# A gated cross-attention block on one core: the third chunk's keys moved ahead of the first slot, and the fourth chunk's transform one slot on

## The chip, the cores and the metric

The kernel runs on one core of one Trainium2 chip. The metric is the device time of one execution in microseconds; before the change it is 108.18 us, the median of three runs (108.13 to 108.33). All stretches of time below are in microseconds from the start of the profiled span.

## What is computed

The input `x` is 8 sequences of 128 tokens with 256 channels. Each token passes two gated branches:

```
x = x + tanh(g_xattn[0]) * wkv(w, u, k=layernorm(x), v=ctx)
x = x + tanh(g_ffn[0])   * ffn(layernorm(x))
```

`wkv` is a recurrence over the 128 tokens of a sequence: a numerator p (decayed sum of exp(k)*v) and a denominator q (decayed sum of exp(k)), and an output y = (A p + E v) / (A q + E). `ffn` applies signs and a normalised Walsh-Hadamard transform to its 256 inputs, multiplies by `W_up` and `W_gate` (1024 x 256 each), forms silu(gate) * up, applies signs and a second Hadamard transform to these 1024 values, and multiplies by `W_down` (256 x 1024).

## The kernel before

**Tiling.** Channels and hidden units lie on the partitions, tokens on the free axis. The 1024 tokens are four chunks of 256 (`NG` = 4, two sequences each), and the 1024 hidden units are eight tiles of 128. A *slot* q is one hidden tile of one chunk, so there are 32 slots; chunk g has the slots 8g to 8g+7. In a slot the PE (TensorE) runs `up(q)` (lines 962 to 1009: 12 matmuls into one PSUM bank, gate and up halves side by side; three products of a high part and a low part in place of one fp32 product), ACT (ScalarE) takes silu of the gate half into S (`gate`, line 636) and, one slot later, the high part of H (`hi`, line 630), DVE (VectorE) multiplies into H (`hidden`, line 815), and POOL (GpSimd) takes the low part HL (line 490). Six slots later (`LAG`) the PE runs `down(q - 6)`, 6 matmuls that add the tile's contribution to the output sums. The banks UG0 to UG3 are used in turn, so `up(q)` waits until H of slot q - 4 is done (`wait_bank_free`, line 275).

**What comes before a chunk's slots.** For each chunk: the layer norm of X (`stats1`, `rstd1` on POOL at line 456, `norm1`), `keys` (PE turns the normalised X and adds a term linear in time, lines 851 to 875; ACT takes exp of the result, line 561), two scans on DVE (line 683), the quotient, x1 = x + branch (line 777), the transform F of x1 (`fwht` on the PE, lines 925 to 943, from the high and low parts XH and XL of x1), squares on ACT, their sum over the channels (`sum` on POOL at line 483, `ones` on the PE at lines 944 to 960, into VB), an inverse square root RR by Ln and Exp on ACT (`rstd2`), a Newton step on DVE in VB whose last operation writes RB (`root`, lines 780 to 788), and F scaled by RB (`f_scaled`, line 792), of which ACT takes the high part FH (line 628) and DVE the low part FL (line 797). `up` of the chunk's first slot waits for FH and FL. The first chunk's `y_part` at line 895 stands for its transform. The scaled F lies in PSUM, its left half in the right half of VB and its right half in FX (`scaled`, line 338).

**Other steps near the change.** `w n` turns a piece of the weights into UGn (line 917), `w_hi` and `w_rest`, `w_lo` split it into two parts (lines 587, 924, 591); `m a` transforms a piece of the down weights into KZ, VB or OD (line 908), from pieces that POOL prepared (`fly`, line 387). `warm` and `warm_ug` are matmuls whose result nobody reads.

**What sets the order.** Four tables (`PE_STAGES` and so on, lines 44 to 102) list by hand which steps each engine issues after which slot; -1 is the part before slot 0. Each engine issues in that order and waits on semaphores. In the table a step is a name and a number: a chunk for `keys`, `fwht`, `ones`, `square`, `sum`, `norm1`; a piece for `w`, `m`. On ACT the Ln and Exp of a chunk stand in an `exp_block` with a table load ahead (line 575) and one behind (line 578), since silu needs another table.

Of the kernel before, what the change touches and what calls it, by code (L numbers as in the profile page):

```python
# [14 lines left out]
CT = C // P  # L15
# [3 lines left out]
GT = GB * P  # L19
# [23 lines left out]

PE_STAGES = {
    -1: [("warm", 9), ("keys", 0), ("warm", 5), ("center", 0), ("w", 0), ("warm", 1), ("x_part", 0), ("w", 1), ("w_rest", 0), ("w", 2),
        ("y_part", 0), ("keys", 1), ("ones", 0), ("w_rest", 1), ("w", 3), ("w_rest", 2), ("m", 0), ("warm_ug", 1)],
    0: [("w_rest", 3)],
    1: [("keys", 2), ("m", 1)],
    2: [("m", 2)],
    3: [("m", 3), ("fwht", 1)],  # L50
    4: [("keys", 3), ("ones", 1)],
    9: [("fwht", 2)],
    12: [("ones", 2)],
    17: [("fwht", 3)],
    19: [("ones", 3)],
}
ACT_STAGES = {
    -1: [("setup", 0), ("own", 0), ("decay", 0), ("signs", 0), ("keys", 0), ("weighted", 0), ("signs", 1), ("ratio", 0), ("negative", 0), ("minus", 1),
        ("center", 0), ("recip", 0), ("w_hi", 0), ("norm1", 1), ("w_hi", 1), ("w_lo", 0), ("w_hi", 4), ("square", 0), ("keys", 1), ("minus", 2), ("w_hi", 2),
        ("rstd2", 0), ("w_lo", 1), ("w_hi", 3), ("w_lo", 2), ("f_hi", 0), ("m_hi", 0), ("norm1", 2), ("recip", 1), ("w_hi", 5), ("w_lo", 3), ("keys", 2)],  # L60
    1: [("m_hi", 1), ("w_hi", 6), ("x_hi", 1)],
    2: [("m_hi", 2), ("w_hi", 7)],
    3: [("m_hi", 3), ("square", 1)],
# [2 lines left out]
    9: [("square", 2)],  # L66
    12: [("exp_block", (("rstd2", 2), ("recip", 3))), ("f_hi", 2)],
    15: [("x_hi", 3)],
    17: [("square", 3)],
    19: [("exp_block", (("rstd2", 3),)), ("f_hi", 3)],  # L70
}
DVE_STAGES = {
    -1: [("stats1", 0), ("setup_rows", 0), ("norm1", 0), ("setup_shift", 0), ("stats1", 1), ("outs", 0), ("scan_a", 0),
# [12 lines left out]
    12: [("root", 2), ("f_scaled", 2), ("f_lo", 2), ("estimate", 3)],  # L86
    13: [("newton", 3), ("x1", 3)],
    15: [("x_lo", 3)],
    19: [("root", 3), ("f_scaled", 3), ("f_lo", 3)],
}  # L90
POOL_STAGES = {
    -1: [("rstd1", 0), ("rstd1", 1), ("fly", 0), ("mix_den", 0), ("fly", 1), ("error", 0), ("fly", 4), ("fly", 2), ("fly", 3), ("fly", 6), ("rstd1", 2),
# [5 lines left out]
    6: [("x1_first", 0)],  # L98
    8: [("sum", 2)],
    11: [("error", 3)],  # L100
    17: [("sum", 3)],
}


# [42 lines left out]
def build(nc, x, xt, ct, rows, consts, weights, w_down, out):  # L147
    with ExitStack() as stack:
# [57 lines left out]
        UG = [bank(f"UG{i}") for i in range(NBANKS)]  # L206
        OD = bank("OD")
        KZ = bank("KZ")
        FX = bank("FX")
        VB = bank("VB")  # L210
# [126 lines left out]

        def scaled(g, t):

            return (FX if t else VB)[:, GT:2 * GT]  # L340

        def normalise(eng, g, done):

# [311 lines left out]
        def _(dve):  # L655
# [32 lines left out]
            def stage(name, g):  # L688
# [24 lines left out]
                elif name == "norm1":  # L713
                    normalise(dve, g, by_dve["norm1"])
                elif name == "av":
                    multiply_values(dve, g, by_dve["av"])
                elif name == "scan_a":
                    dve.wait_ge(decay_set, CT)
                    dve.wait_ge(pads, 2)
                    if g:  # L720
                        dve.wait_ge(den_ready, g)
                    dve.wait_ge(a_ready, g + 1)
                    scan(SQ, g, OD[:, :] if g in HELD else EA[:, g - len(HELD), :, :, :].rearrange("p t b q -> p (t b q)"), scanned_a)
                elif name == "scan_av":
                    if g:
                        dve.wait_ge(num_ready, g)
                    wait_shared(dve, "av", g)
                    scan(SP_, g, OD[:, :] if g in HELD else V[:, g, :, :, :].rearrange("p t b q -> p (t b q)"), scanned_v)
                elif name == "mix_den":
                    if g == 2:  # L730
                        dve.wait_ge(y_first, CT)
                    elif g > 2:
                        dve.wait_ge(y_ready, g - 2)
                    dve.wait_ge(scanned_a, 2 * g + 2)
                    for t in range(CT):
                        i = dve.scalar_tensor_tensor(out=DEN[:, g % 2, t, :, :], in0=exps(g)[:, t, :, :], scalar=RATIO[:, t:t + 1],
                                                     in1=states(SQ)[:, t, :, :], op0=ALU.mult, op1=ALU.add)
                    i.then_inc(den_ready, 1)
                elif name == "mix_num":
                    if g == 0:  # L740
                        dve.wait_ge(ratio_ready, 1)
                    dve.wait_ge(scanned_v, 2 * g + 2)
                    num = values(g)
                    for t in range(CT):
                        i = dve.scalar_tensor_tensor(out=num[:, t, :, :], in0=num[:, t, :, :], scalar=RATIO[:, t:t + 1],
                                                     in1=states(SP_)[:, t, :, :], op0=ALU.mult, op1=ALU.add)
                    i.then_inc(num_ready, 1)
                elif name == "error":
                    reciprocal_error(dve, g, by_dve["error"])
                elif name == "estimate":  # L750

                    dve.wait_ge(r0_ready, g + 1)
                    dve.wait_ge(num_ready, g + 1)
                    if g:
                        dve.tensor_tensor(lanes(values(g)), lanes(values(g)), lanes(R0[:, g % 2, :, :, :]), ALU.mult).then_inc(y0_ready, 1)  # L755
                    else:
                        dve.wait_ge(tanh_gate, 1)
                        dve.scalar_tensor_tensor(out=lanes(values(g)), in0=lanes(values(g)), scalar=TG[:, 0:1], in1=lanes(R0[:, g % 2, :, :, :]),
                                                 op0=ALU.mult, op1=ALU.mult).then_inc(y0_ready, 1)
                elif name == "newton":  # L760

                    wait_shared(dve, "error", g)
                    dve.wait_ge(y0_ready, g + 1)
                    if g:
                        dve.scalar_tensor_tensor(out=lanes(values(g)), in0=lanes(DEN[:, g % 2, :, :, :]), scalar=2.0, in1=lanes(values(g)),
                                                 op0=ALU.subtract, op1=ALU.mult).then_inc(y_ready, 1)
                    else:
                        for t in range(CT):
                            dve.scalar_tensor_tensor(out=YT[:, t, :].rearrange("p (b q) -> p b q", b=GB), in0=DEN[:, 0, t, :, :], scalar=2.0,
                                                     in1=values(g)[:, t, :, :], op0=ALU.subtract, op1=ALU.mult).then_inc(y_first, 1)  # L770
                elif name == "x1":

                    dve.wait_ge(y_ready, g)
                    dve.wait_ge(tanh_gate, 1)
                    dve.wait_ge(xt_in[arrival(g)], 16)
                    xg = XT[:, g, :, :].rearrange("p t (b q) -> p (t b) q", q=P)
                    dve.scalar_tensor_tensor(out=xg, in0=lanes(values(g)), scalar=TG[:, 0:1], in1=xg, op0=ALU.mult, op1=ALU.add).then_inc(x1_ready, 1)
                elif name == "x_lo":
                    split_x1(dve, g, by_dve["x_lo"])
                elif name == "root":  # L780

                    var = VB[:, 0:GT]
                    dve.wait_ge(rr_ready, g + 1)
                    dve.scalar_tensor_tensor(out=var, in0=var, scalar=EPS * C, in1=RR[:, :], op0=ALU.add, op1=ALU.mult).then_inc(e_ready, 1)
                    dve.wait_ge(e_ready, 3 * g + 1)
                    dve.tensor_tensor(var, var, RR[:, :], ALU.mult).then_inc(e_ready, 1)
                    dve.wait_ge(e_ready, 3 * g + 2)
                    dve.scalar_tensor_tensor(out=RB[:, :], in0=var, scalar=3.0, in1=RR[:, :], op0=ALU.subtract, op1=ALU.mult).then_inc(e_ready, 1)
                elif name == "f_scaled":
                    dve.wait_ge(e_ready, 3 * g + 3)  # L790
                    for t in range(CT):
                        dve.scalar_tensor_tensor(out=scaled(g, t), in0=FX[:, t * GT:(t + 1) * GT], scalar=-0.5, in1=RB[:, :],
                                                 op0=ALU.mult, op1=ALU.mult).then_inc(f_scaled, 1)
                elif name == "f_lo":
                    for t in range(CT):
                        dve.wait_ge(f_hi, CT * g + t + 1)
                        dve.tensor_tensor(FL[:, g, t, :], scaled(g, t), FH[:, g, t, :].bitcast(F32), ALU.subtract).then_inc(f_lo, 1)
                elif name == "fly":
                    fly(dve, g, by_dve["fly"])
                elif name == "w_lo":  # L800
                    split_weight(dve, g, by_dve["w_lo"])
                elif name == "m_lo":
                    dve.wait_ge(m_hi, M_HI.index(g) + 1)
                    dve.tensor_tensor(m_part(ML, g), fill(("m", g))[:, :], m_part(MH, g).bitcast(F32), ALU.subtract).then_inc(by_dve["m_lo"], 1)
# [36 lines left out]
        def _(pe):  # L841
            def stage(name, g):
# [8 lines left out]
                elif name == "keys":  # L851
# [5 lines left out]
                    else:  # L857
                        pe.wait_ge(a_ready, g)
                    if g == 2:
                        pe.wait_ge(f_lo, CT)  # L860
                    elif g == 3:
                        wait_shared(pe, "m_lo", M_FULL[1])
                    keys = VB if g == 2 else KZ
# [234 lines left out]
```

## Time and profile before

| | |
|---|---|
| runs | 108.13, 108.18, 108.33 us |
| the profiled execution | 108.13 us; its span 106.2 us |
| PE busy | 100.4 us (94%), 724 matmul records |
| weight load (PEld) | 91.3 us (86%) |
| DVE | 70.0 us (66%) |
| ACT | 68.4 us (64%) |
| POOL | 62.4 us (59%) |
| PE's share of the chain that ended last | 60% |
| mean granted TensorE clock | 0.999 of 2.4 GHz |

An engine's rows give the start and the duration; of several merged instructions the duration reaches from the first start to the last end. Matmuls overlap their neighbours, so the time that one takes from the PE is the distance between starts, not its duration.

### The profile page before, as it was taken

To read this page: it belongs to the slowest core of one execution; us is meant where nothing else is said; L and a number is where in the kernel's file an instruction comes from. 1 tells how busy PE (TensorE), PEld (TensorE's weight loads), DVE (VectorE), ACT (ScalarE), POOL (GpSimd) and SP (SyncE) were. 2 spreads that over 40 slices of the span, in tenths; PEclk is the share of its full clock that TensorE was granted. 3 is DMA by queue.
4 is the path that set the end of the run, shared out by engine and by line. 5 is a ranking of instruction groups with operands and counts; after the bars stand their busy time and mean duration, and the time that the engine had idled before them with its cause. 6 is when DMAs were issued, how large, how long until landed. Compare 5 with 4: busy or idle time off the path is not lost.

```text
span 106.2 us, 2028 instructions
## 1 busy us (share of the span) xinstructions
PE 100.4 (94%) x724; PEld 91.3 (86%) x724; DVE 70.0 (66%) x151; ACT 68.4 (64%) x153; POOL 62.4 (59%) x74
## 2 busy tenths in 40 slices
PE   6999999989999999988999999799999999999990
PEld 5778778659667999978999999699999999999980
DVE  0388889799899996898998269942298231125221
ACT  4098797989979699925346997565976432443400
POOL 7025999996999995049996345455208234225500
PEclk9999999999999999999999999999999999999999
DMA  1999999300000000000000000020000200000202
GB/s 59 271 348 398 413 413 405 147 0 9 0 0 0 0 6 0 0 0 3 0 0 6 0 0 0 0 105 0 0 0 3 99 6 0 0 0 3 99 6 99
DMA packets 2893, 7.70 MB, mean 72 GB/s; under 512 B 321, under 2 KB 706, under 8 KB 2754
## 3 DMA queue, kind: packets, MB, share of 16 engines
q1 hardware_dynamic: 2882, 7.56, 19.0%
q8 instruction: 6, 0.10, 0.4%
q14 instruction: 5, 0.04, 0.1%
HBM read 6.51 MB, written 1.05 MB: 71 GB/s over the span
## 4 chain that ended last, share of the span: by engine, by line
PE 60%; DVE 13%; ACT 9%; issue 6%; POOL 5%; DMA 3%; DVEq 0%; ACTq 0%; POOLq 0%
PE UG L978 33%; PE OD L1016 8%; DMA X<-in_x 3%; PE KZ L1016 3%; PE FX L941 3%; PE VB L1016 3%; PE FX L1016 3%; PE FX L895 2%; DVE XL L377 2%; PE KZ L908 2%; PE OD L908 2%; PE VB L908 2%; DVE BS L706 1%; POOL RS L456 1%; DVE V L755 1%
## 5 line engine op out<-in xcount | busy, mean ns | idle before, releaser
L490 POOL TENSOR_TENSOR HL<-H,HH 128x256 fp32r<-128x256 f32 x32 | 25.5, 805 | 27.5 <-ACT HH L634 27.5
L826 DVE SCALAR_TENSOR_TENSOR H<-S,ALPHA,UG 128x256 f32<-128x256 f32 x32 | 15.0, 476 | 16.7 <-ACT S L643 16.6
L643 ACT ACTIVATE S<-UG,HI 128x256 f32<-128x256 f32 x32 | 15.0, 471 | 13.7 <-PE UG L978 13.7
L978 PE MATMUL UG<-FH,WTH 128*128 128x256 f32 x128 | 21.7, 292 | 0.8 <-DVE H L826 0.5
L634 ACT ACTIVATE HH<-H 128x256 fp32r<-128x256 f32 x32 | 13.2, 414 | 10.9 <-DVE H L826 10.9
L978 PE MATMUL UG<-FH,WTL 128*128 128x256 f32 x128 | 19.9, 278 | 0.0
L978 PE MATMUL UG<-FL,WTH 128*128 128x256 f32 x128 | 19.9, 278 | 0.0
L978 PEld LDWEIGHTS UG<-FH,WTH 128*128 128x128 f32 x128 | 17.6, 188 | 2.6 <-issue 1.7
L978 PEld LDWEIGHTS UG<-FH,WTL 128*128 128x128 f32 x128 | 17.1, 188 | 0.0
L978 PEld LDWEIGHTS UG<-FL,WTH 128*128 128x128 f32 x128 | 17.0, 188 | 0.0
L849 PE MATMUL VB<-ONES 128*128 128x256 f32 x30 | 10.0, 499 | 1.0 <-POOL ONES L439 1.0
L849 PEld LDWEIGHTS VB<-ONES 128*128 128x128 f32 x30 | 7.5, 260 | 2.5 <-POOL ONES L439 1.0
L1016 PE MATMUL OD<-HL,MH 128*128 128x256 f32 x32 | 8.9, 278 | 0.0
L1016 PE MATMUL OD<-HH,ML 128*128 128x256 f32 x32 | 8.9, 278 | 0.0
L1016 PE MATMUL OD<-HH,MH 128*128 128x256 f32 x32 | 8.9, 278 | 0.0
L364 POOL TENSOR_TENSOR DEN<-DEN,R 128x512 f32<-128x512 f32 x4 | 5.1, 1283 | 4.7 <-ACT R L572 4.7
L456 POOL TENSOR_TENSOR RS<-VE,NHALF 128x2 f32<-128x2 f32 x4 | 2.8, 704 | 5.8 <-DVE VE L712 5.8
L370 POOL TENSOR_TENSOR WTL<-WN,WTH 128x512 fp32r<-128x512 f32 x4 | 6.1, 1517 | 0.0
L1016 PEld LDWEIGHTS OD<-HL,MH 128*128 128x128 f32 x32 | 6.0, 189 | 0.0
L1016 PEld LDWEIGHTS OD<-HH,ML 128*128 128x128 f32 x32 | 6.0, 188 | 0.0
L1016 PEld LDWEIGHTS OD<-HH,MH 128*128 128x128 f32 x32 | 6.0, 188 | 0.0
L706 DVE BATCH_NORM_STATS2 BS<-X 128x6 f32<-128x256 f32 x8 | 3.0, 414 | 4.2 <-DMA X<-in_x 4.2
(159 smaller groups left out, 221.6 us busy)
## 6 DMA issues: line engine op xcount, KB each, us to landing
WN<-in_weights SPq DMA_DIRECT2D x4, 512.0 KB, 9.2
DN<-in_w_down SPq DMA_DIRECT2D x1, 1024.0 KB, 6.8
out<-XT SPq DMA_DIRECT2D x3, 256.0 KB, 2.5
X<-in_x SPq DMA_DIRECT2D x2, 256.0 KB, 3.8
V<-in_ct SPq DMA_DIRECT2D x2, 256.0 KB, 7.7
XT<-in_xt SPq DMA_DIRECT2D x2, 256.0 KB, 9.3
X<-in_x SPq DMA_DIRECT2D x1, 512.0 KB, 9.3
V<-in_ct SPq DMA_DIRECT2D x1, 512.0 KB, 11.7
```

What stands on the lines that cost most here:

```text
L364: eng.tensor_tensor(lanes(DEN[:, g % 2, :, :, :]), lanes(DEN[:, g % 2, :, :, :]), lanes(R0[:, g % 2, :, :, :]), ALU.mult).then_inc(done, 1)
L370: eng.tensor_tensor(w_part(WTL, n), src, w_part(WTH, n).bitcast(F32), ALU.subtract).then_inc(done, 1)
L456: pool.tensor_tensor(RS1[:, GB * g:GB * (g + 1)], VE1[:, GB * g:GB * (g + 1)], NHALF[:, :], ALU.pow).then_inc(rstd1, 1)
L490: pool.tensor_tensor(HL[:, q % JT, 0:n], ring(H, q), HH[:, q % JT, 0:n].bitcast(F32), ALU.subtract).then_inc(h_lo, 1)
L634: act.activation(HH[:, q % JT, 0:n], ring(H, q), ACT.Copy).then_inc(h_hi, 1)
L643: act.activation(ring(S, q), gate_part(q), ACT.Silu, scale=VT[:, V_SGATE + j:V_SGATE + j + 1]).then_inc(silu_ready, 1)
L706: dve.bn_stats(BS1[:, n, :], X[:, n, :]).then_inc(stats1, 1)
L826: dve.scalar_tensor_tensor(out=ring(H, q), in0=ring(S, q), scalar=ALPHA[:, j:j + 1], in1=up_part(q), op0=ALU.mult, op1=ALU.mult).then_inc( ...
L849: pe.matmul((VB if name == "warm" else UG[1])[:, 0:WARM].rearrange("p (k q) -> p k q", q=P), ONES[:, :], ONES[:, :].unsqueeze(1).broadcast ...
L908: a = pe.matmul(fill(item)[:, :], had, DN[:, n:n + 2, :].rearrange("p j c -> p (j c)"), start=(i == 0), stop=(i == 1), skip_group_check=True)
L978: return pe.matmul(dst.rearrange("p (g n) -> p g n", n=GT), w[:, m, j, t, :], f[:, chunks, t, :], start=start, stop=stop, skip_group_check ...
L1016: a = pe.matmul(total(g, t), m[:, j, t * P:(t + 1) * P], h[:, j, 0:n], start=(j == 0 and k == 0 and (t == 0 or g == LAST)), stop=(j == JT ...
```

## The change

It does four things. (1) On the PE, `keys` of the third chunk (number 2) moves from behind slot 1 to ahead of slot 0, the matmul `warm_ug` is gone, and `m 0` goes ahead of `w_rest 2`. On ACT, the normalisation of that chunk (`norm1` 2) moves from behind `m_hi 0` to directly behind `w_lo 1`, and `w_hi 3` and `w_lo 2` move behind `m_hi 0`. (2) The scaled F of the first chunk has its left half in UG1 in place of VB, and DVE waits for `w_lo` 1 before it writes there. (3) The keys of the third chunk wait for the end of the first chunk's Newton step (`e_ready` 3) in place of its low part FL. (4) The fourth chunk's `fwht`, `square` and `sum` go from behind slot 17 to behind slot 18, its `ones`, exponentials, Newton step, scaling and splits from behind slot 19 to behind slot 20.

```diff
 PE_STAGES = {
     -1: [...
-        ("y_part", 0), ("keys", 1), ("ones", 0), ("w_rest", 1), ("w", 3), ("w_rest", 2), ("m", 0), ("warm_ug", 1)],
+        ("y_part", 0), ("keys", 1), ("ones", 0), ("w_rest", 1), ("w", 3), ("m", 0), ("w_rest", 2), ("keys", 2)],
     0: [("w_rest", 3)],
-    1: [("keys", 2), ("m", 1)],
+    1: [("m", 1)],
...
-    17: [("fwht", 3)],
-    19: [("ones", 3)],
+    18: [("fwht", 3)],
+    20: [("ones", 3)],
 ACT_STAGES = {
...
-        ("rstd2", 0), ("w_lo", 1), ("w_hi", 3), ("w_lo", 2), ("f_hi", 0), ("m_hi", 0), ("norm1", 2), ("recip", 1), ("w_hi", 5), ("w_lo", 3), ("keys", 2)],
+        ("rstd2", 0), ("w_lo", 1), ("norm1", 2), ("f_hi", 0), ("m_hi", 0), ("w_hi", 3), ("w_lo", 2), ("recip", 1), ("w_hi", 5), ("w_lo", 3), ("keys", 2)],
...
-    17: [("square", 3)],
-    19: [("exp_block", (("rstd2", 3),)), ("f_hi", 3)],
+    18: [("square", 3)],
+    20: [("exp_block", (("rstd2", 3),)), ("f_hi", 3)],
 DVE_STAGES = {
...
-    19: [("root", 3), ("f_scaled", 3), ("f_lo", 3)],
+    20: [("root", 3), ("f_scaled", 3), ("f_lo", 3)],
 POOL_STAGES = {
...
-    17: [("sum", 3)],
+    18: [("sum", 3)],
...
         def scaled(g, t):
-            return (FX if t else VB)[:, GT:2 * GT]
+            if t:
+                return FX[:, GT:2 * GT]
+            return VB[:, GT:2 * GT] if g else UG[1][:, 0:GT]
...
                 elif name == "f_scaled":
                     dve.wait_ge(e_ready, 3 * g + 3)
+                    if g == 0:
+                        wait_shared(dve, "w_lo", 1)
...
                     if g == 2:
-                        pe.wait_ge(f_lo, CT)
+                        pe.wait_ge(e_ready, 3)
```

The PE's instructions from behind `w 3` to the start of slot 0, before:

```order
L924 MATMUL UG<-WTH,NI 128x512 [waits ni_ready,w_hi]
L908 MATMUL KZ<-DN,HI 128x512 [waits const_in,fly_pool,a_ready]
L908 MATMUL KZ<-DN,HI 128x512
L849 MATMUL UG<-ONES 128x256 [waits w_lo_act,ones_set]
L978 MATMUL UG<-FH,WTH 128x256 [waits f_hi,w_hi,w_lo_act]
```

and with the change (all lines of the kernel's code there are four further on):

```order
L912 MATMUL KZ<-DN,HI 128x512 [waits const_in,fly_pool,a_ready]
L912 MATMUL KZ<-DN,HI 128x512
L928 MATMUL UG<-WTH,NI 128x512 [waits ni_ready,w_hi]
L872 MATMUL VB<-HI,X 128x128 [waits norm1_act,e_ready,a_ready]
L872 MATMUL VB<-HI,X 128x128 x3
L878 MATMUL VB<-STEPR,WPLUS 128x256 x2
L982 MATMUL UG<-FH,WTH 128x256 [waits f_hi,w_hi,w_lo_act]
```

The four transposes and two matmuls of the keys now stand between `w_rest 2` and slot 0, where one matmul of ones stood, and the first of them waits for ACT's normalisation.

ACT from `w_lo 1` on, before:

```order
L591 ACTIVATE WTL<-UG 128x512
L587 ACTIVATE WTH<-UG 128x512
L591 ACTIVATE WTL<-UG 128x512
L628 ACTIVATE FH<-VB 128x256
L628 ACTIVATE FH<-FX 128x256
L595 ACTIVATE MH<-KZ 128x512
L547 ACTIVATE NMR<-NM,RS 128x1 x2
L551 ACTIVATE X<-X,NMR,RS 128x256 x2
L570 ACTIVATE R<-DEN 128x512
```

and with the change:

```order
L593 ACTIVATE WTL<-UG 128x512
L549 ACTIVATE NMR<-NM,RS 128x1 x2
L553 ACTIVATE X<-X,NMR,RS 128x256 x2
L630 ACTIVATE FH<-UG 128x256
L630 ACTIVATE FH<-FX 128x256
L597 ACTIVATE MH<-KZ 128x512
L589 ACTIVATE WTH<-UG 128x512
L593 ACTIVATE WTL<-UG 128x512
L572 ACTIVATE R<-DEN 128x512
```

The normalisation (NMR, X) and the two weight steps (WTH, WTL) have changed places around FH and MH.

The PE between slots 17 and 18, from the last matmul of `down(11)`, before:

```order
L1016 MATMUL KZ<-HL,MH 128x256
L941 MATMUL FX<-XH,AT 128x256 x4
L941 MATMUL FX<-XL,AT 128x256 x4
L978 MATMUL UG<-FH,WTH 128x256 x4
L978 MATMUL UG<-FH,WTL 128x256 x4
L978 MATMUL UG<-FL,WTH 128x256 x4
```

and with the change:

```order
L1020 MATMUL KZ<-HL,MH 128x256
L982 MATMUL UG<-FH,WTH 128x256 x4
L982 MATMUL UG<-FH,WTL 128x256 x4
L982 MATMUL UG<-FL,WTH 128x256 x4
L1020 MATMUL KZ<-HH,MH 128x256
```

The eight matmuls of the fourth chunk's transform now follow `up(18)` and `down(12)`.

## Rows read from the trace of the kernel before

**Rows 1.** The chain that ended last, in order of time: start, us, what.

```profile
22.05 0.44 DVE VB L792
...
24.70 0.23 PE UG L924
...
37.35 0.12 ACT S L643
```

**Rows 2.** Timeline of PE, 20 to 28: start, us, instruction [idle before <-releaser].

```profile
20.32 1.96 PE L908 MATMUL KZ<-DN,HI 128*128 128x512 f32 x4
22.11 0.59 PE L849 MATMUL UG<-ONES 128*128 128x256 f32 x2
23.04 0.74 PE L978 MATMUL UG<-FH,WTH 128*128 128x256 f32 x4 [0.34 <-ACT FH L628]
23.62 0.62 PE L978 MATMUL UG<-FH,WTL 128*128 128x256 f32 x4
...
26.18 0.60 PE L868 MATMUL VB<-HI,X 128*128 128x128 f32 x4
...
26.86 1.88 PE L908 MATMUL KZ<-DN,HI 128*128 128x512 f32 x4
```

**Rows 3.** Timeline of ACT, 21 to 25.

```profile
21.01 0.59 ACT L587 ACTIVATE WTH<-UG 128x512 fp32r<-128x512 f32 x1
...
22.52 0.38 ACT L628 ACTIVATE FH<-VB 128x256 fp32r<-128x256 f32 x1 [0.43 <-DVE VB L792]
...
23.61 0.47 ACT L547 ACTIVATE NMR<-NM,RS 128x1 f32<-128x1 f32 x2
23.97 1.08 ACT L551 ACTIVATE X<-X,NMR,RS 128x256 f32<-128x256 f32 x2
```

**Rows 4.** Timeline of POOL, at 20.

```profile
20.18 0.70 POOL L456 TENSOR_TENSOR RS<-VE,NHALF 128x2 f32<-128x2 f32 x1
```

**Rows 5.** Timeline of PE, 46 to 48.

```profile
46.95 0.74 PE L978 MATMUL UG<-FH,WTH 128*128 128x256 f32 x4 [0.47 <-DVE H L826]
47.52 0.62 PE L978 MATMUL UG<-FH,WTL 128*128 128x256 f32 x4
```

**Rows 6.** Timeline of DVE, 38 to 57.

```profile
38.69 1.58 DVE L745 SCALAR_TENSOR_TENSOR V<-V,RATIO,SP_ 128x256 f32<-128x256 f32 x2
...
41.59 0.43 DVE L784 SCALAR_TENSOR_TENSOR VB<-VB,RR 128x256 f32<-128x256 f32 x1 [0.92 <-ACT RR L624]
...
56.11 0.88 DVE L745 SCALAR_TENSOR_TENSOR V<-V,RATIO,SP_ 128x256 f32<-128x256 f32 x2
```

**Rows 7.** Timeline of PE, 67 to 73.

```profile
67.82 0.28 PE L1016 MATMUL KZ<-HL,MH 128*128 128x256 f32 x1
68.79 0.71 PE L941 MATMUL FX<-XH,AT 128*128 128x256 f32 x4 [0.70 <-ACT XH L601]
...
70.12 0.63 PE L978 MATMUL UG<-FH,WTH 128*128 128x256 f32 x4
...
72.17 0.62 PE L978 MATMUL UG<-FH,WTH 128*128 128x256 f32 x4
```

**Rows 8.** Timeline of DVE, at 67: H of slot 14.

```profile
67.21 0.47 DVE L826 SCALAR_TENSOR_TENSOR H<-S,ALPHA,UG 128x256 f32<-128x256 f32 x1
```

**Rows 9.** Timelines of POOL, PE and DVE, 73 to 83: the fourth chunk's sums, F, first slot.

```profile
73.30 0.74 POOL L483 TENSOR_TENSOR FSUM<-FSQ 128x256 f32<-128x256 f32 x1
...
74.21 0.64 PE L954 MATMUL VB<-FSUM,ONES 128*128 128x256 f32 x2
...
79.46 0.42 DVE L797 TENSOR_TENSOR FL<-FX,FH 128x256 fp32r<-128x256 f32 x1
...
82.88 0.62 PE L978 MATMUL UG<-FH,WTH 128*128 128x256 f32 x4
```

**Rows 10.** Timeline of PE, 0 to 8; then one line's records (ns min/median/max).

```profile
0.98 7.09 PE L849 MATMUL VB<-ONES 128*128 128x256 f32 x18 [0.98 <-POOL ONES L439]
...
L849 PE MATMUL UG<-ONES x2: 379/380/380, 22.1 to 22.3; 128*128 128x256 f32 x2
```

## The prediction

> **What bounds the kernel now.** The page first: the PE is busy for 94% of the span, and the slices where it is not are few. So the question at each place is whether the PE waits, and for whom. The chain that ended last answers it. Up to 22.5 it runs through DVE and ACT (the Newton step, then F scaled at 22.05, [rows 1]), and the PE is the one that waits: it stands idle for 0.34 us before slot 0, released by FH [rows 2]. From 23.04 the chain is the PE's alone until it reaches ACT's silu of slot 4 at 37.35 [rows 1]. There ACT has to get slot 4's gate before it may load the exp table, and the second chunk's F, and behind it everything up to about 50, hangs on that. From about 51 on it is the PE again, save for one wait: behind slot 17 the PE issues its last matmul at 67.82 and the next only at 68.79, because the fourth chunk's transform needs XH [rows 7]. After 70.12 the PE never waits.
>
> Hence two places at which the time can be moved: the work in the PE's queue between 23.04 and 37, where every microsecond taken out brings slot 4 forward, and the wait at 67.9.
>
> **Keys of the third chunk ahead of slot 0.** Their six instructions (the four transposes and two matmuls, of more records in the trace) take the PE from 26.18 to 26.86, 0.68 us, all of it on the chain [rows 2]. They leave that place. In the new place they follow `m 0` and `w_rest 2`. `m 0` cannot start earlier than its 20.32, as it did not wait for `w_rest 2` but for POOL's last piece, which ended when POOL began the next operation at 20.18, about 0.1 earlier [rows 2, 4]; it holds the PE until 22.11, and `w_rest 2` takes 0.23 as its neighbour does [rows 1, 2], so the PE is free at 22.34. The keys must also wait for ACT. ACT is free for the normalisation at 21.01, where `w_hi 3` started [rows 3]; its inputs from POOL are there at 20.18 + 0.70 = 20.88 [rows 4]. It takes 25.05 - 23.61 = 1.44 us [rows 3], to 22.45. FH started at 22.52 after an idle time of 0.43 [rows 3], so the normalisation just fits ahead of it, and FH is not late: what hides it is that idle time plus the 1.07 of the two weight steps that moved behind. The Newton step is done at 22.05, so the new wait of the keys on it costs nothing.
>
> From ACT's end to the PE's start the trace has 0.14 us (FH ends at 22.90, the PE starts at 23.04 [rows 2, 3]). The keys start at 22.45 + 0.14 = 22.59. A stream of matmuls that starts after idling loses something more: the first four of slot 9 took 0.57 [rows 5], where 18 matmuls of a slot take 72.17 - 70.12 = 2.05, so 0.114 each and 0.46 for four [rows 7]. That is 0.11 for a start, and it lies between 0 and 0.11 here, as the PE has idled for only 0.25 us. I take the 0.11, since slot 9's start, the nearest row, carries it. Then slot 0 starts at 22.59 + 0.68 + 0.11 = 23.38, against 23.04. It no longer pays for its own start: its first four took 23.62 - 23.04 = 0.58 [rows 2] and now take 0.46. So the PE is 0.34 - 0.12 = 0.22 late into slot 0 and 0.68 early behind slot 1: **0.46 us** gained, between 0.45 and 0.59. `warm_ug` stood in the PE's wait for FH (its start at 22.11 [rows 2]), and its removal brings nothing by itself.
>
> Does the gain reach the end? Between 26.2 and 37.3 the trace shows no wait of the PE, and with the queue 0.46 earlier the releases that I followed are still in time: DVE's XL of the second chunk by about 0.5 us, ACT's `w_hi 3`, now behind `m_hi 0`, by about 0.3 us before `w_rest 3`. Slot 4's silu comes 0.46 earlier, ACT's exp block with it, and DVE, which idled 0.92 us for RR at 41.59 [rows 6], has 0.46 of that left. From there on all is released by that chain, so it shifts as a whole.
>
> POOL gets its share earlier too, since ACT reaches the second chunk's reciprocal about 0.4 us sooner, and POOL's operations then lie otherwise beside DVE's. The same pair of DVE operations took 1.58 us at 38.69 and 0.88 at 56.11 [rows 6]; the difference of 0.70 bounds what a collision with POOL costs, and gain and loss are both open, from -0.70 to +0.70. Up to 0.46 of a loss goes into the idle time before 41.59, so at most 0.24 would be seen; I take nothing, as the pair at 38.69 bears its collision already. The Trainium skill (SBUF — State Buffer, Who interferes with whom) says that a DVE instruction with two SBUF inputs and a reading GpSimd instruction lock each other out for a whole instruction, by issue order. By that rule one more instruction of POOL in the way could cost its full length and would be seen as the same 0.2 to 0.3 us; the doubled pair agrees with it.
>
> **F's left half in UG1.** The same DVE and ACT operations on another PSUM bank, and a wait on `w_lo 1`, which ACT had all but ended when its next operation started at 21.01 [rows 3], while F is scaled at 22.05 [rows 1]: nothing. It is what makes VB free for the keys in time.
>
> **The fourth chunk's transform a slot on.** Behind `down(11)` the PE is free at 67.82 + 0.11 = 67.93, and slot 18 starts at 70.12: 2.19 us, of which eight matmuls at 0.114 need 0.91 [rows 7]. The rest, **1.28 us**, is the wait for XH and then XL. In the new order `up(18)` comes first. It waits for H of slot 14, done at 67.21 + 0.47 = 67.68 [rows 8], 0.25 before the PE is free, and a release by DVE is seen some 0.05 later. The transform starts at 67.93 + 2.05 = 69.98, when XH and XL have long been there: before, all of it had been issued by 70.12. So the whole 1.28 goes, if nothing else comes late.
>
> What is late next? Sums: the PE's `ones` follows the transform by two slots before and now, and POOL's sum by the same steps, done at 74.04 for a start at 74.21 [rows 9]; the margin of 0.17 stays. The F of the fourth chunk: the `ones`, and ACT's and DVE's block, come one slot (2.05) later and 1.28 earlier, so 0.77 later: FL at 79.46 + 0.42 + 0.77 = 80.65. Slot 24 now asks for it at 82.88 - 1.28 = 81.60 [rows 9]. 0.95 us are left. ACT's silus of slots 21 to 23 wait behind the block instead of 20 to 22, and the PE asks for slot 21's H only at slot 25. No DMA is moved, and no instruction but the matmul of ones is added or removed.
>
> **The sum.** 0.46 + 1.28 = 1.74. The profiled execution took 108.13 us, 1.9 more than its span, and 0.05 below the median; 108.13 - 1.74 = 106.39, against the median 106.44. I say **106.4 us**.
>
> **The rivals.**
>
> *The first gain is lost.* The keys wait for ACT, and everything of slot 0 stands behind them. If the normalisation ended 0.5 later (its inputs late from POOL, or ACT held), slot 0 would be late by what the keys save. For: POOL's value comes 0.13 before ACT wants it. Against: nothing moves on POOL or ACT ahead of it. It gives 108.13 - 1.28 = 106.9.
>
> *The second change does not do what it says.* `up(18)` trades the wait for XH for a wait for H of slot 14; both come out of the same DVE sequence. For: the margin is only 0.25. Against: both sides shift together, since both hang on the chain through ACT. If DVE were late by 1.3 the time would be 108.13 - 0.46 = 107.7.
>
> *The PE slows down: the slower side.* The first matmuls of ones stand 7.09 / 18 = 0.39 apart [rows 10], those at 22.11 only 0.21 (0.59 for both [rows 2] less 0.38 for one [rows 10]), 1.9 times as fast, though the granted clock reads 1.00 for both stretches. The change puts a gap at 20 and one at 22.4 around transposes and takes a plain matmul out. If that brought the slow pace back at slot 0, the stretch 23.04 to 26.18 [rows 2] would take 1.9 times as long, 2.8 us more, and the time would be 109.2. It decides against the change from about 2 us of such work on. Against it: the PE has idled longer at 46.95 and 68.79 and its spacing behind stayed 0.114. The Trainium skill (TensorE: Matmul & The Clock Gate, PE-mode transpose) says that transposes do not count as PE activity in the way other matmuls do, which speaks for this rival. By it, the time would again be this 109.2; the trace, with transposes at 26.18 and full pace behind them, does not bear it out.
>
> **Chances.** The forecast 0.82, the first gain lost 0.07, the second 0.05, the slow pace 0.03, no change at all (both) 0.03. A measurement of this kernel tells about 0.2%, 0.2 us, from no change. Faster: 0.82 + 0.07 + 0.05 = 0.94; same 0.03; slower 0.03. The forecast's own range is 106.1 to 106.7 (0.13 from the gap, 0.24 from collisions, and some for other margins); with the first rival it goes to 107.0, and I open it down to 106.0.
>
> **What the new profile would show.** The keys in VB at about 22.6, slot 0 at 23.4, `m 1` directly behind slot 1 at about 26.4; FH still at 22.5; the exp block of ACT at 37.7; no idle time of the PE for XH, `up(18)` at 67.5 and the transform at 69.5; slot 24 at about 81.1 without a wait; `ones` of the fourth chunk unstalled. The prediction is wrong if the PE waits at the keys beyond 22.7, at `up(18)`, at the fourth chunk's `ones`, or at slot 24.

## The result, and the profile after

The changed kernel takes 106.60 us, the median of four runs (106.44 to 106.79), where the kernel before takes 108.25 us beside it. The ratio is 0.985, with a 95% interval of 0.9825 to 0.9874: faster by 1.6 us. In another series of runs (a job: several kernels run by turns) the ratio was 0.986 (0.981 to 0.991). The forecast was 106.4 us, in a range of 106.0 to 107.0.

The profiled execution took 106.77 us with a span of 104.9. First the PE's timeline around slot 0, with the columns of [rows 2]:

```profile
20.50 1.96 PE L912 MATMUL KZ<-DN,HI 128*128 128x512 f32 x4 [0.30 <-issue]
...
22.78 0.63 PE L872 MATMUL VB<-HI,X 128*128 128x128 f32 x4
23.17 0.48 PE L878 MATMUL VB<-STEPR,WPLUS 128*128 128x256 f32 x2
23.49 0.63 PE L982 MATMUL UG<-FH,WTH 128*128 128x256 f32 x4
...
25.13 0.63 PE L982 MATMUL UG<-FH,WTH 128*128 128x256 f32 x4
...
26.55 1.88 PE L912 MATMUL KZ<-DN,HI 128*128 128x512 f32 x4
```

The keys stand at 22.78, slot 0 at 23.49, and `m 1` follows slot 1 at 26.55; in [rows 2] it followed the keys at 26.86. ACT in the same stretch, against [rows 3]:

```profile
21.18 0.47 ACT L549 ACTIVATE NMR<-NM,RS 128x1 f32<-128x1 f32 x2
21.56 1.08 ACT L553 ACTIVATE X<-X,NMR,RS 128x256 f32<-128x256 f32 x2
22.69 0.39 ACT L630 ACTIVATE FH<-UG 128x256 fp32r<-128x256 f32 x1
```

The normalisation ends at 22.64, 0.14 ahead of the keys and 0.05 ahead of FH, which it doesn't delay. The PE behind slot 17, against [rows 7]:

```profile
67.60 0.62 PE L982 MATMUL UG<-FH,WTH 128*128 128x256 f32 x4
...
69.64 0.64 PE L945 MATMUL FX<-XH,AT 128*128 128x256 f32 x4
70.12 0.63 PE L945 MATMUL FX<-XL,AT 128*128 128x256 f32 x4
70.59 0.62 PE L982 MATMUL UG<-FH,WTH 128*128 128x256 f32 x4
...
74.67 0.64 PE L958 MATMUL VB<-FSUM,ONES 128*128 128x256 f32 x2
...
81.30 0.62 PE L982 MATMUL UG<-FH,WTH 128*128 128x256 f32 x4
```

No row carries an idle time (the PE waits for nothing there): slot 18 at 67.60, the transform in 0.95, slot 19 at 70.59, slot 24 at 81.30. The waits of the PE, all of them over the span (engine, line, what for: us in total, times, longest):

```profile
PE VB L853 <- POOL ONES L441: 1.0, 1, 1.0
PE UG L982 <- DVE H L830: 0.5, 1, 0.5
PE KZ L912 <- issue: 0.3, 1, 0.3
PE FX L899 <- DVE YT L771: 0.3, 1, 0.3
PE FX L945 <- DVE XL L379: 0.3, 1, 0.3
```

The wait for XH (0.70 in [rows 7]) and that for FH (0.34 in [rows 2]) are gone.

**How to compare two traces here.** Everything up to slot 0 depends on how fast the inputs arrive, and POOL, ACT and DVE were 0.17 to 0.18 later in this execution from the first loads on. So I count from the start of the first chunk's FH on ACT. Neither half of the change moves it: it stands 2.83 us behind the start of ACT's first step of the first chunk's RR before, and 2.82 with the change. Slot starts of the PE, in us behind it:

| kernel | FH at | slot 0 | slot 4 | slot 9 | slot 17 | slot 19 | slot 31 |
|---|---|---|---|---|---|---|---|
| before | 22.52 | 0.52 | 13.20 | 24.43 | 43.37 | 49.65 | 74.64 |
| changed | 22.69 | 0.80 | 12.73 | 23.96 | 42.87 | 47.90 | 72.89 |

The changed kernel gains 0.47 by slot 4, holds it to slot 17 (0.50), and gains 1.25 between slots 17 and 19 (6.28 against 5.03). At slot 31 it stands at 1.75 us; the forecast's sum was 1.74. Of that, the profiled execution shows 1.36 in its time, since it began 0.17 later and its last store took 0.3 longer (its wait for the last DMA was 1.8 us against 1.5).

### The profile page after: what moved, and what is told of

The parts are those of the page before. It is cut to its first block, busy times and chain, and to the rows that moved or that the text cites. A ratio compares the mean times of both kernels' runs of the same rounds, so it can differ in the third digit from the quotient of the medians.

```text
span 104.9 us, 2024 instructions
## 1 busy us (share of the span) xinstructions
PE 99.3 (95%) x722; PEld 90.7 (86%) x722; DVE 70.0 (67%) x151; ACT 68.3 (65%) x153; POOL 62.7 (60%) x74
## 4 chain that ended last, share of the span: by engine, by line
PE 52%; DVE 18%; ACT 10%; DMA 7%; issue 6%; POOL 3%; SPq 2%; DVEq 0%
PE UG L982 29%; PE OD L1020 8%; DMA DN<-in_w_down 7%; PE KZ L1020 5%; DVE XL L379 3%; PE VB L1020 3%; PE FX L1020 3%; DVE SQ L685 2%; PE FX L899 2%; PE FX L945 2%; DVE DEN L738 2%; DVE FL L801 1%; POOL DEN L463 1%; ACT R L572 1%; POOL DEN L366 1%
```

## The experiments

**The two halves.** Each alone, made by putting the other back:

```diff
 keys_only: the fourth chunk's steps where they were
-    18: [("fwht", 3)],   20: [("ones", 3)],
+    17: [("fwht", 3)],   19: [("ones", 3)],
     (and so for square, sum, rstd2, f_hi, root, f_scaled, f_lo)
 fourth_only: the kernel before, with
-    17: [("fwht", 3)],   19: [("ones", 3)],
+    18: [("fwht", 3)],   20: [("ones", 3)],
     (and so for the same steps)
```

> Only the first half of the change: keys of the third chunk ahead of slot 0 and F's left half in UG1; the fourth chunk's steps stay where they were. If the two halves are independent and worth 0.46 and 1.28 us, the time is 108.25 - 0.46 = 107.8 us, the keys start about 0.14 us behind ACT's normalisation, and the PE waits 0.7 us for XH behind slot 17 again. Rival: the first half alone is lost further on (ACT's or DVE's chain takes it back before slot 9), then it is 108.2 us.

> Only the second half: the fourth chunk's transform, sums and exponentials a slot on; everything ahead of slot 17 as before. Theory: 108.25 - 1.28 = 107.0 us, with no wait of the PE between slots 17 and 31. Rival (the margins behind it are used up, or the wait for XH becomes one for H of slot 14): over 107.3 us.

Keys alone: ratio 0.9954 (0.992 to 0.9987). The fourth chunk alone: 0.988 (0.979 to 0.997). The time of the kernel before was 109.25 us in this job, so the forecasts in us can't be held against it; the ratios are what was expected (0.9957 and 0.988). Both were run again beside the changed kernel:

> Only the third chunk's keys ahead of slot 0, again, at the pace of this chip: 0.45 to 0.5 us under the kernel before (ratio 0.9956). With the half above it adds up to the whole change. Rival: it is lost behind slot 9, and the difference is under 0.2 us.

> Only the fourth chunk's steps a slot on, again, at the pace of this chip: 1.2 to 1.3 us under the kernel before (ratio 0.988). Rival, if the first half works only together with it or the pace changed its worth: under 1.0 us.

> The changed kernel again, beside its two halves and the version with DVE's long steps moved, on one chip. The traces so far show the PE at two paces, 0.113 and 0.117 us a matmul, with the same granted clock, and the kernel before at 108.2 or at 109.25 us by the pace of its last twenty slots. If that is all that differs between chips, the change takes the same 1.6 to 1.8 us from either: 106.5 to 106.6 where the kernel before takes 108.25, 107.5 to 107.7 where it takes 109.25. Rival: at the slow pace part of the gain is lost, under 1.3 us.

| kernel | median us | ratio, 95% interval | FH to slot 4 | slots 17 to 19 | FH to slot 31 |
|---|---|---|---|---|---|
| keys_again | 107.71 | 0.995 (0.992 to 0.998) | 12.73 | 6.28 | 74.23 |
| fourth_again | 108.05 | 0.991 (0.987 to 0.996) | 13.22 | 5.18 | 73.62 |
| after_again | 106.75 | 0.986 (0.981 to 0.991) | 12.68 | 5.03 | 72.87 |
| (before) | 108.39 | | 13.20 | 6.28 | 74.64 |
| keys_only, first job | 108.76 | 0.9954 (0.992 to 0.9987) | 12.69 | 6.36 | 75.07 |
| fourth_only, first job | 108.27 | 0.988 (0.979 to 0.997) | 13.20 | 5.03 | 73.37 |

The row of the kernel before has the median of this job, but its distances are from its only trace. keys_only comes to slot 31 later than the kernel before did in that trace, though it gained its 0.5 us by slot 4: its PE took 25.87 us from slot 19 to slot 31 in place of 24.99, a slower pace without a wait (the last section has more on it).

The traces separate the halves cleanly: the keys give 0.47 by slot 4 and nothing between 17 and 19, the fourth chunk the reverse. In the trace of keys_again the old wait is back:

```profile
68.70 0.71 PE L945 MATMUL FX<-XH,AT 128*128 128x256 f32 x4 [0.56 <-ACT XH L603]
```

In fourth_again, the fourth chunk alone came out at 1.02 at slot 31 in place of 1.25. Between slots 17 and 19 its PE took about 0.118 us a matmul in place of 0.114: 44 matmuls lie between these two starts, and the 0.15 between 5.18 and 5.03 is 44 times 0.0035. Another 0.07 had been lost by slot 17. Its medians differ by only 0.34 us (108.39 against 108.05), and its ratio of 0.991 is worth 0.9 us, where 1.2 to 1.3 were expected. The expected 0.988 is inside the interval, but so is the rival, under 1.0 us. What this half is worth in us thus rests on the traces, and the runs don't exclude that it is less at the slow pace. The changed kernel met its expectation in the ratio. Two of its six runs took 107.60 and 107.69 us, 1.6 below the group of the kernel before at 109.16 to 109.45, which speaks against a smaller gain at the slow pace; none of these executions has a trace.

**Who sets slot 0.** ACT's normalisation put back behind `m_hi 0`, the rest of the change kept:

```diff
-("w_lo", 1), ("norm1", 2), ("f_hi", 0), ("m_hi", 0), ("w_hi", 3), ("w_lo", 2), ("recip", 1)
+("w_lo", 1), ("w_hi", 3), ("w_lo", 2), ("f_hi", 0), ("m_hi", 0), ("norm1", 2), ("recip", 1)
```

> The changed kernel with ACT's order as it was before: the third chunk's normalisation behind m_hi 0 again. Theory: the keys and slot 0 hang on ACT's normalisation, which then ends at about 25.1 us; slot 0 starts at about 26.0 in place of 23.4, 2.6 us late, and all of it reaches the end: 109.2 us. Rival: the PE has slack behind slot 0 (DVE and ACT set the pace up to slot 4 by themselves), then much less than 2.6 us is lost, 107.5 us or less.

111.9 us, ratio 1.024 (1.016 to 1.032): 2.6 us slower than the kernel before, far more than I expected. Two things were not in my sum. The first is on ACT:

```profile
21.04 0.59 ACT L589 ACTIVATE WTH<-UG 128x512 fp32r<-128x512 f32 x1
22.59 0.60 ACT L593 ACTIVATE WTL<-UG 128x512 fp32r<-128x512 f32 x1 [0.96 <-PE UG L928]
23.08 0.38 ACT L630 ACTIVATE FH<-UG 128x256 fp32r<-128x256 f32 x1
```

`w_lo 2` now waits 0.96 us for `w_rest 2`, which the change put behind `m 0` on the PE, and FH comes 0.5 us late. So the change had to move `w_lo 2` behind FH in any case, not only to make room for the normalisation. The second is the PE:

```profile
25.70 1.09 PE L872 MATMUL VB<-HI,X 128*128 128x128 f32 x4 [3.15 <-ACT X L553]
27.01 1.05 PE L982 MATMUL UG<-FH,WTH 128*128 128x256 f32 x4
...
29.37 0.64 PE L982 MATMUL UG<-FH,WTH 128*128 128x256 f32 x4
```

and its granted clock in windows of one microsecond (columns: window, then busy us and count of PE, weight load, DVE, ACT, POOL, the granted clock, DMA share, GB/s):

```profile
24.00:25.00 1.00, 0.00 (x0) 0.00 (x0) 1.00 (x4) 1.00 (x5) 1.00 (x2) 1.00 0.02 8
25.00:26.00 1.00, 0.30 (x2) 0.33 (x3) 1.00 (x3) 1.00 (x3) 0.27 (x1) 0.59 0.00 0
26.00:27.00 1.00, 1.00 (x6) 1.00 (x5) 0.90 (x2) 0.97 (x3) 0.18 (x1) 0.50 0.06 16
...
28.00:29.00 1.00, 1.00 (x8) 1.00 (x7) 0.90 (x3) 0.00 (x0) 1.00 (x2) 0.70 0.00 0
29.00:30.00 1.00, 1.00 (x10) 0.96 (x9) 0.89 (x2) 0.43 (x1) 0.34 (x1) 1.00 0.00 0
```

The PE issued no matmul for 3.15 us. Then the clock is at 0.50, the 1.2 GHz level, and it is back at 2.4 GHz from 29 on. From the keys to slot 1 the PE took 29.37 - 25.70 = 3.67 us, against 25.13 - 22.78 = 2.35 in the changed kernel: 1.3 us more, at the low clock. By slot 4 this kernel is 4.4 us behind the changed one (19.30 against 14.92 behind the start of `m 0`), of which 0.5 is FH's delay, 1.3 the clock and 2.6 the normalisation as expected.

**F's left half back in VB.**

```diff
-            return VB[:, GT:2 * GT] if g else UG[1][:, 0:GT]
+            return VB[:, GT:2 * GT]
...
-                    if g == 0:
-                        wait_shared(dve, "w_lo", 1)
...
-                        pe.wait_ge(e_ready, 3)
+                        pe.wait_ge(f_lo, CT)
```

> The changed kernel with F's left half in VB again, so the keys must wait for FL of the first chunk, as before. FL ends at 23.7 us in the trace before; keys from 23.75, slot 0 at 24.5 in place of 23.4: 1.15 us lost, 107.75 us, so the keys would then be worth less than nothing (their 0.46 becomes a loss of 0.7). Rival: the bank does not matter, 106.6 us.

```profile
24.03 0.63 PE L870 MATMUL VB<-HI,X 128*128 128x128 f32 x4 [1.28 <-DVE FL L799]
```

Slot 0 started at 24.74, 1.98 behind FH in place of 0.80: 1.18 late, against 1.15 expected, and 1.14 of it still stood at slot 4. The ratio is 0.997 (0.994 to 1.000), about 1.2% above that of the changed kernel, which is 1.3 us. As expected: the other bank is what makes the early keys worth having. At slot 4 this kernel is 0.67 behind the kernel before (13.87 against 13.20), the forecast's loss of 0.7.

**A filler matmul kept.** One matmul of ones between `w_rest 2` and the keys. It writes UG0 and waits for `w_lo` 0, since UG1 now holds F:

```diff
-("m", 0), ("w_rest", 2), ("keys", 2)]
+("m", 0), ("w_rest", 2), ("warm_ug", 1), ("keys", 2)]
...
-                        wait_shared(pe, "w_lo", 1)
+                        wait_shared(pe, "w_lo", 0)
     (and UG[0] in place of UG[1])
```

> The changed kernel with one matmul of ones kept, between w_rest 2 and the keys, into UG0. If a start after idling costs the PE 0.11 us, the filler (0.42 us from 22.34) takes the gap's place and ends 0.17 after the keys could start, but saves the 0.11: the same within 0.1 us, 106.6. If the PE's pace fell for want of the filler, this is faster by over 0.5 us, about 106. If the gap costs nothing it is 0.17 slower.

```profile
22.66 0.59 PE L853 MATMUL UG<-ONES 128*128 128x256 f32 x2
23.09 0.60 PE L872 MATMUL VB<-HI,X 128*128 128x128 f32 x4
23.45 0.48 PE L878 MATMUL VB<-STEPR,WPLUS 128*128 128x256 f32 x2
23.77 0.63 PE L982 MATMUL UG<-FH,WTH 128*128 128x256 f32 x4
```

Ratio 0.988 (0.987 to 0.989); the changed kernel has 0.985 and 0.986. Slot 0 comes 0.95 behind FH in place of 0.80, so the filler costs 0.15, nearly the 0.17 of "the gap costs nothing". The keys' first four matmuls took 0.36 here and 0.39 behind the gap: this start cost 0.03 us, not 0.11. And the pace did not need the filler: from slot 0 to slot 4 the PE took 11.89 us with it and 11.93 without.

**Two slots on.** The fourth chunk's steps at 19 and 21:

> The changed kernel with the fourth chunk's transform, square, sum, ones and exponentials two slots on in place of one (19 and 21). Theory: the wait for XH is already gone with one slot, so the second gives nothing, and F comes 2.05 us later: FH of the fourth chunk is then some 0.8 us late for slot 24, and the time is 106.6 + 0.9 = 107.5 us, with a wait of the PE for FH ahead of slot 24. Rival: the margin of 0.95 us at slot 24 that I reckoned is too small a figure and nothing waits: 106.6 us.

```profile
82.07 0.74 PE L982 MATMUL UG<-FH,WTH 128*128 128x256 f32 x4 [0.15 <-ACT FH L630]
```

107.69 us, ratio 0.9865 (0.985 to 0.988). The wait for FH is there, ahead of slot 24, and the profile shows no other from slot 10 on. Its price is not what I expected: 0.9 us would be a ratio 0.008 above the changed kernel's 0.985 or 0.986, and it is above by less than 0.002.

The reserve that I had reckoned, 0.95 us, was that of FL, and slot 24 doesn't begin with FL. Its first matmuls need FH, and FL is asked for only by its third group. In the changed kernel:

```profile
79.15 0.38 ACT L630 ACTIVATE FH<-VB 128x256 fp32r<-128x256 f32 x1 [0.59 <-DVE VB L796]
79.91 0.42 DVE L801 TENSOR_TENSOR FL<-FX,FH 128x256 fp32r<-128x256 f32 x1
82.20 0.62 PE L982 MATMUL UG<-FL,WTH 128*128 128x256 f32 x4
```

The first half of FH is done at 79.53 and the PE could start 0.14 later; slot 24 starts at 81.30, so the reserve is 1.63. FL is done at 80.33, 0.97 before slot 24 (forecast: 0.95) but 1.87 before it is asked for. In two_on this FH starts 2.50 later behind the first chunk's FH, and the PE is free for slot 24 at 81.75, 0.56 later than the changed kernel's slot 24, as it did slots 17 to 23 at the slow pace: 2.50 - 1.63 - 0.56 = 0.31, and the PE waits from 81.75 to 82.07. The start behind the wait costs it another 0.12 (the first four matmuls took 0.58 in place of 0.46).

**The third chunk's transform a slot on too.**

```diff
-    9: [("fwht", 2)],
+    10: [("fwht", 2)],
```

> The changed kernel with the third chunk's transform on the PE one slot on (behind slot 10), all else in place. The PE's wait for XL behind slot 9 goes, about 0.55 us there. Theory: that stretch is set by DVE and ACT, not by the PE, so the third chunk's F comes no sooner and the gain is given back at slot 16: at most 0.2 us, 106.4 to 106.6. Rival: the PE bounds, as at the fourth chunk: 106.05 us.

```profile
51.11 0.64 PE L945 MATMUL FX<-XH,AT 128*128 128x256 f32 x4
...
63.72 0.71 PE L982 MATMUL UG<-FH,WTH 128*128 128x256 f32 x4 [0.30 <-ACT FH L630]
```

The wait for XL is gone and a wait for FH has come at slot 16, which starts 40.75 behind the first FH in both kernels. The whole gain is given back there. The ratio, 0.983 (0.979 to 0.986), doesn't part the two: the time is not shown to differ from the changed kernel's. ACT's exp block for the third chunk begins 35.50 behind the first FH in the changed kernel and 35.51 here, so the freed PE moves nothing on ACT. That it is DVE that holds ACT there is what the next experiment tests.

**DVE's long steps moved behind what the PE waits for**, together with the edit above:

```diff
-    4: [..., ("estimate", 2), ("newton", 2)],   5: [("x1", 2)],
-    6: [("x_lo", 2), ("scan_a", 3)],
-    8: [("mix_den", 3), ("scan_av", 3)],   9: [("mix_num", 3)],
-    12: [("root", 2), ...
+    4: [..., ("estimate", 2)],   5: [("newton", 2), ("x1", 2)],
+    6: [("x_lo", 2)],   7: [("scan_a", 3)],
+    8: [("mix_den", 3)],   9: [("scan_av", 3)],
+    12: [("mix_num", 3), ("root", 2), ...
```

> As the one with the third chunk's transform behind slot 10, and DVE's long steps moved behind the products that the PE waits for: newton 2 behind H of slot 5, scan_a 3 behind slot 7, scan_av 3 behind slot 9, mix_num 3 into DVE's idle time ahead of root 2. H of slots 5 and 7 to 11 come 0.8 to 1.7 us earlier, ACT's exp block of slot 12 starts 0.8 earlier. Theory (DVE sets this stretch): 0.8 to 1.2 us faster, 105.4 to 105.8. Rival (the PE is full there anyway): 106.4 to 106.6.

> The version with newton 2, scan_a 3, scan_av 3 and mix_num 3 of DVE moved back and the third chunk's transform behind slot 10, again: its trace shows no wait of the PE behind slot 0. 1.1 to 1.3 us under the changed kernel in the same job, 2.8 us under the kernel before (ratio 0.974).

Ratios 0.974 (0.973 to 0.975) and 0.968 (0.964 to 0.973) against the kernel before; in the second job 105.14 us where the changed kernel has 106.75. Behind slot 0 the PE never waits, neither at slot 9 nor for XL:

```profile
46.18 0.63 PE L983 MATMUL UG<-FH,WTH 128*128 128x256 f32 x4
...
48.30 0.63 PE L983 MATMUL UG<-FH,WTH 128*128 128x256 f32 x4
...
50.42 0.63 PE L946 MATMUL FX<-XH,AT 128*128 128x256 f32 x4
```

The rows are of dve_again. ACT's exp block begins 33.65 behind the first FH there and 33.72 in dve_late, 1.8 earlier than in the changed kernel, so DVE's order did hold it. Slot starts behind the first FH:

| kernel | slot 11 | slot 17 | from 11 to 17 |
|---|---|---|---|
| changed | 29.72 | 42.87 | 13.15 |
| dve_late | 28.60 | 41.75 | 13.15 |
| dve_again | 28.46 | 41.28 | 12.82 |

The moved steps and the two waits that they remove are worth 1.12 and 1.26 at slot 11, about the upper end of the 0.8 to 1.2 that I expected. dve_again gains 0.33 more up to slot 17, because its PE went through these slots at the fast pace, 2.04 us a slot in place of 2.12. In the changed kernel such a pace brings nothing there: keys_again did slots 10 and 11 at 2.04 each, and its slot 16 starts at 40.74 all the same, since FH comes no sooner. That makes the 1.6 us between the medians of the second job, above my 1.1 to 1.3. This version beats both kernels.

## Why the prediction was right

**What bounds the kernel** held at both places that the change touches. The PE's queue between slot 0 and slot 4 sets that stretch: work taken out of it reaches slot 4, ACT's exp block and the end. And the wait behind slot 17 was the only one of the last twenty slots. One sentence did not hold: "From about 51 on it is the PE again". Up to slot 16 the PE is full, but FH of the third chunk comes at the same moment. In the changed kernel its first half is done at 63.28 and slot 16 starts at 63.44, the distance that a start behind FH has at slot 0 too (0.14), and neither third_on, which takes out a wait of the PE ahead of it, nor a faster pace moves that slot. The trace before has the same: 63.61 and 63.76. It did no harm to the sum, since the 0.46 of slot 4 goes through ACT and DVE as well and moves both limits.

**The keys.** The term was 0.46 and the trace shows 0.47 at slot 4 (0.47 in keys_again). Its parts: the keys start 0.14 behind the normalisation, as forecast from FH to slot 0 (their 22.78 is 22.60 in the time of the trace before, which ran 0.18 earlier, so the sign of being wrong, a wait beyond 22.7, did not come); slot 0 comes 0.28 later behind FH than before (forecast 0.34); the stretch from slot 0 to slot 1 is 1.64 in place of 1.73 (forecast 0.12 less, measured 0.09); 0.67 go from behind slot 1. One size was off: "I take the 0.11" for the start after the gap. It was 0.03, shown by the keys' first four matmuls with the gap and without. The reason is not that the gap was short: behind the 1.28 us of f_in_vb the keys lost 0.03 too (0.39), while slot 24 of two_on lost 0.12 behind 0.3 us. The nearest row was one of another kind of matmul, 256 columns wide, and the keys begin with transposes of 128. It cost little, because the saving at slot 0 and the keys' length were each overrated by 0.01 to 0.03.

**That the normalisation just fits** was right, by 0.05 us. What the text gave as its cover was incomplete. It counted the two weight steps behind FH as room for the normalisation; norm_late showed that `w_lo 2` had to go there anyway, since `w_rest 2` now ends at about 22.5. Had it stayed, FH would have been about 0.5 late, by norm_late's rows.

**DVE's reserve.** "0.46 of that left" of the idle time before the second chunk's Newton step:

```profile
41.28 0.43 DVE L786 SCALAR_TENSOR_TENSOR VB<-VB,RR 128x256 f32<-128x256 f32 x1 [0.41 <-ACT RR L626]
```

It was 0.41. The pair of DVE operations that stood for a collision with POOL took 1.60 in place of 1.58 [rows 6]: nothing, as I took it. POOL's two operations beside it didn't come earlier: they start at 37.11 and 39.27 against 36.91 and 39.07. So no run here tests the Trainium skill's rule of the lock (SBUF — State Buffer, Who interferes with whom) any further: it would have allowed 0.2 to 0.3 us of loss, and none shows.

**The fourth chunk.** 1.28 forecast, 1.25 measured, and 1.25 again with this half alone at the same pace (fourth_only: slot 19 at 70.89 and slot 17 at 65.86, 5.03). The margins came out as worked: H of slot 14 is done at 67.36 for slot 18 at 67.60 (0.24, forecast 0.25), POOL's sum at 74.50 for 74.67 (0.17), FL at 80.33 against the start of slot 24 at 81.30 (0.97, forecast 0.95). The last was well reckoned and the wrong one to reckon, as two_on showed: slot 24 starts on FH, whose reserve is 1.63. The forecast lost nothing by it, since either is enough.

**The rivals.** The first, a lost first gain, did not come, but norm_late is that rival made true. The second did not come either (H of slot 14 is done 0.24 ahead). The third, a slow PE from slot 0 on, did not come: slots 0 to 4 took 11.93 us, 0.75 less than before: 0.67 for the keys and the rest for the start at slot 0. The PE can fall to half its clock, but it did so after 3.15 us without a matmul and not at gaps of 0.3 us among transposes, and there the granted clock shows it, which it did not in the slow stretch of [rows 10]. Through the keys, six matmuls of which four are transposes, the changed kernel's granted clock stays at 1.00. The Trainium skill says that transposes don't count as PE activity in the way other matmuls do (TensorE: Matmul & The Clock Gate, PE-mode transpose). This trace neither bears it out nor refutes it: the keys' 0.71 us stand among other matmuls. norm_late's low clock came with no matmul of any kind ahead of it, so it doesn't test it either.

**What was not in the sum:** the 0.4 us between 1.75 gained on the engines and 1.36 in the profiled time, from the inputs and the last store. The median shows 1.65.

## What to carry to other kernels

Read a wait of the busiest engine together with what stands next in its queue: if the next piece has its inputs, put it first, and the wait is worth its whole length (1.25 us here), as long as every user of what was put back has the reserve, counted step by step to the matmul that really waits for it (at slot 24 FH, not FL). Where the engine waits in front of a piece that everything needs, as at slot 16, moving the queue only moves the wait, and the gain lies in the other engine's order (1.1 to 1.3 us for four steps of DVE, and 0.3 more where the PE ran at its faster pace). Take the price of a start from a row of the same kind of matmul. And compare traces from an instant that the change can't touch.

## What the runs showed of the hardware

- The PE has two paces at one granted clock. Four matmuls of 256 columns stand 0.45 or 0.47 us apart, 0.113 or 0.117 us each, while the clock column reads 1.00 for both. In the trace before it was the slower one from 51 to 64 and the faster one from 70 on; in keys_only it was the slower one from 70 to the end. A slot then takes 2.12 us in place of 2.04, and the stretch from slot 19 to slot 31 takes 25.87 in place of 24.99, 0.9 us more, which is more than half of what this change is worth. It may be why the kernel before is at 108.25 us in one job and at 109.25 in another; no trace of it at 109.25 was kept, so that is not shown. What sets the pace was not found; no step of the kernel lines up with its start or its end.
- After 3.15 us without a matmul the granted clock was 0.50 for nearly 3 us of work, which cost 1.3 us on top of the wait.
- In these rows, what a start after a wait costs the PE went by the kind of matmul and not by the length of the gap; why was not tested. The keys' four transposes of 128 columns lost 0.03 us behind 0.25 us (changed kernel) and behind 1.28 us (f_in_vb: 0.39 in place of 0.36). Four matmuls of 256 columns lost 0.11 to 0.12 at slot 9 behind 0.54 us (46.65 to the next group at 47.23, less 0.46) and at slot 24 of two_on behind 0.3 us (82.07 to 82.65).
